# First attention of a decoder layer: keys and values laid out block-diagonally over 64 rows by 64 columns, multiplied in two row strips, with a new job order

## The reference

```python
Q, K, V = proj(Wq, bq), proj(Wk, bk), proj(Wv, bv)   # (n, s, h, d), h = d = 16, after reshape and transpose
scores = jnp.einsum('nqhd,nkhd->nhqk', Q, K) * scale
attn = jax.nn.softmax(scores, axis=-1)
out = jnp.einsum('nhql,nlhd->nqhd', attn, V)
...
x = _layernorm(x + attn_1(x))
x = _layernorm(x + cross_attn(ctx, ctx, x))
x = _layernorm(x + ffn_block(x))                       # attention over the sequence, then 8 experts, top 2
```

## Time and profile before

| | before |
|---|---|
| median of 3 runs | 1203.14 us |
| the profiled execution | 1210.79 us, span 1209.0 us |
| mean granted TensorE clock in it | 0.956 |
| PE / PEld busy | 1082.4 us (90%) / 1015.5 us (84%) |
| DVE, ACT, POOL busy | 810.2, 622.7, 588.4 us |
| first job of phase B on DVE | about 626 us after the start |

### The profile page before, as it was taken

The page is one execution under the profiler, slowest core; times in us unless marked ns, Lnnn a source line. Parts: engine busy times, 40 slices in busy tenths (PEclk is TensorE's granted clock), DMA queues, the critical chain, the costliest instruction groups (busy, mean ns, idle before and its releaser), DMA issues. The chain is left out here.

```text
span 1209.0 us, 32884 instructions
## 1 busy us (share of the span) xinstructions
PE 1082.4 (90%) x13012; PEld 1015.5 (84%) x13012; DVE 810.2 (67%) x1383; ACT 622.7 (52%) x1264; POOL 588.4 (49%) x631
## 2 busy tenths in 40 slices
PE   3799999999999999999728988799999999999981
PEld 2578888899899888898628987799999999999981
DVE  1668877878778778776535432477677767767576
ACT  1245455565555555665422232466666666666443
POOL 4243433433444343334101666267767766766555
PEclk8999999999999999999957988899999999999995
DMA  7585465454555554410058222256766676676265
GB/s 202 97 188 106 80 123 107 90 116 115 108 96 118 116 98 88 86 43 20 28 180 317 88 84 88 100 202 222 244 232 210 226 247 225 217 248 225 86 194 174
DMA packets 288456, 176.37 MB, mean 146 GB/s; under 512 B 213120, under 2 KB 256896, under 8 KB 287680
## 3 DMA queue, kind: packets, MB, share of 16 engines
q1 hardware_dynamic: 277600, 148.90, 46.1%
q0 software_dynamic: 6816, 18.69, 4.3%
q10 hardware_dynamic: 3888, 6.69, 1.5%
HBM read 130.25 MB, written 54.28 MB: 153 GB/s over the span
## 5 line engine op out<-in xcount | busy, mean ns | idle before, releaser
L1395 DVE TENSOR_TENSOR prod<-silu,up 128x512 f32<-128x512 f32 x110 | 75.1, 683 | 161.4 <-ACT silu L1249 139.2
L1379 DVE TENSOR_TENSOR we_lo<-w_raw,we_hi 128x1024 fp32r<-128x1024 f32 x117 | 148.0, 1304 | 15.3 <-ACT we_hi L1233 12.0
L1516 POOL TENSOR_TENSOR act_lo<-prod,act_hi 128x512 fp32r<-128x512 f32 x78 | 100.6, 1290 | 101.5 <-ACT act_hi L1256 101.5
L1524 POOL DMA_INDIRECT routed_scratch<-y_rows,slot_place x78 | 130.9, 1678 | 21.2 <-issue 14.7
L1249 ACT ACTIVATE silu<-gate 128x512 f32<-128x512 f32 x110 | 64.9, 590 | 128.2 <-PE up L1180 98.1
L1233 ACT ACTIVATE we_hi<-w_raw 128x1024 fp32r<-128x1024 f32 x117 | 118.1, 1049 | 21.7 <-DMA w_raw<-in_w_down 21.6
L1256 ACT ACTIVATE act_hi<-prod 128x512 fp32r<-128x512 f32 x110 | 69.6, 632 | 89.4 <-DVE prod L1395 87.5
L668 ACT ACTIVATE p3t<-psum 128x512 f32<-128x512 f32 x128 | 68.7, 596 | 90.8 <-PE psum L517 90.8
L1483 POOL DMA_INDIRECT slots_scratch<-h_rows,slot_index x64 | 65.0, 1016 | 52.5 <-PE up L1180 33.5
L920 POOL TENSOR_TENSOR ctx_lo<-ctx_t,ctx_hi 128x512 fp32r<-128x512 f32 x16 | 20.6, 1286 | 140.3 <-ACT ctx_hi L578 140.3
L839 DVE TENSOR_REDUCE max<-psum 128x16 f32<-128x2048 f32 x32 | 73.3, 2291 | 18.2 <-PE psum L503 18.2
(11 more groups left out here) (264 smaller groups left out, 3322.5 us busy)
## 6 DMA issues: line engine op xcount, KB each, us to landing
w_raw<-in_w_gate SPq DMA_DIRECT2D x40, 512.0 KB
w_raw<-in_w_up SPq DMA_DIRECT2D x40, 512.0 KB
w_raw<-in_w_down SPq DMA_DIRECT2D x40, 512.0 KB
slots_scratch<-in_empty SPq DMA_DIRECT2D x39, 258.0 KB, 3.4
slot_rows<-slots_scratch SPq DMA_DIRECT2D x39, 258.0 KB
w_raw<-routed_scratch SPq DMA_DIRECT2D x32, 256.0 KB, 3.8
x_t<-in_x_t SPq DMA_DIRECT2D x16, 256.0 KB, 3.5
q_scratch<-qk SPq DMA_DIRECT2D x16, 256.0 KB, 2.7
```

Of the source, the lines that this page charges most:

```text
L1379: dve.tensor_tensor(w_lo[:, kind, :], w_raw[:, use % 2, kind, :], w_hi[:, kind, :].bitcast(F32), ALU.subtract).then_inc(w_lo_done, 1)
L1395: dve.tensor_tensor(prod[:, h, :], silu[:, h, :], up[h][:, :], ALU.mult).then_inc(prod_done, 1)
L1516: pool.tensor_tensor(act_lo[:, n % 2, h * FH:(h + 1) * FH, :], prod[:, h, :].rearrange("p (f n) -> p f n", f=FH), act_hi[:, n % 2, h * FH: ...
L1524: pool.indirect_dma_start(out=scratch["routed"], out_offset=bass.IndirectOffsetOnAxis(ap=slot_place[:, i % METAS, j:j + 1], axis=0), in_=y ...
```

## The change

What the diff does, in the first attention alone and in the tables of the order:

1. `kbd` and `vbd` are 64 columns wide instead of 128. Tokens 0 to 3 of a group keep rows 0 to 63 and tokens 4 to 7 rows 64 to 127, and both halves use the same 64 columns.
2. `s1_0` and `s1_1` become one job `s1`, and `o1_0` and `o1_1` one job `o1`. Each has 64 matmuls of 64 rows, 32 stationary columns and 64 streamed columns, in the two strips of 64 rows times four strips of 32 columns. The two row strips write to two different PSUM banks.
3. The evictions follow: `max1`, `sub1`, `o1e` now go by half of a group (a bank) instead of by sequence, with the same number of elements each, and write `p1` in the old layout through a strided view. `exp1`, `t1`, `den1`, `to1` still go by sequence, so each of them waits for both halves.
4. The memsets of `kbd` and `vbd` at the start are half as large, and that of `v3` too (one copy instead of two).
5. `SCHEDULE`, `BANK` and `BUFS` are new for all jobs of phase A. The total lag is the same (7), and PE's largest lag is 6 in both.

```diff
-    for r in range(4):                                      # s1_0, s1_1; the same shape in o1_0, o1_1
-        for j in range(4):
-            g = GB1 * a + 4 * r + j
-            mm = pe.matmul(dst[32 * j:32 * (j + 1), r * P:(r + 1) * P], qc[:, g, :], kbd[:, g, :],
-                           start=True, stop=True)
+    for i in range(2 * 4):                                  # s1; the same shape in o1
+        for half in range(2):
+            for j in range(4):
+                rows, cols = slice(HALF * half, HALF * (half + 1)), 512 * half + HALF * i
+                mm = pe.matmul(dst[32 * j:32 * (j + 1), cols:cols + HALF], qc[rows, 4 * i + j, :],
+                               kbd[rows, 4 * i + j, :], start=True, stop=True)
...
-        kbd = sb("kbd", [P, 2 * GB1, P])
-        vbd = sb("vbd", [P, 2 * GB1, P])
+        kbd = sb("kbd", [P, 2 * GB1, TH * DH])
+        vbd = sb("vbd", [P, 2 * GB1, TH * DH])
...
-                        after(act, f"sub1_{a}", pair)
+                        after(act, "sub1_1", pair)
...
-                        after(pe, f"o1e_{a}", pair)
+                        after(pe, "o1e_1", pair)
...
-BUFS = {"ctx_t": 2, "x_res": 1, "x1": 1, "vo": 1, "x2": 5, "v3": 2}
+BUFS = {"ctx_t": 3, "x_res": 3, "x1": 5, "vo": 2, "x2": 2, "v3": 1}
...
-    "sp": [("load_ctx", 3), ("store_v1", 2), ("store_sum", 7), ("load_k1", 2), ("load_q1", 2), ("load_v1", 2),
-        ("store_q1", 1), ("load_x", 0), ("load_res", 2), ("store_h2", 6), ("store_l", 7)],
+    "sp": [("load_ctx", 2), ("load_x", 0), ("load_v1", 2), ("store_q1", 1), ("store_h2", 6), ("load_res", 0),
+        ("store_v1", 1), ("store_sum", 5), ("store_l", 7), ("load_q1", 1), ("load_k1", 1)],
```

More of the change, by code:

```diff
@@ L96 @@
 }
+TH, HALF = T1 // 2, P // 2
 FAMILIES = [
@@ L101 @@
     ("q3", "k3"), ("q3_0e", "q3_1e", "k3_0e", "k3_1e"),
-    *((f"{n}_0", f"{n}_1") for n in ("s1", "max1", "sub1", "exp1", "den1", "t1", "t1e", "o1", "o1e", "to1", "o1hi", "o1lo",
+    *((f"{n}_0", f"{n}_1") for n in ("max1", "sub1", "exp1", "den1", "t1", "t1e", "o1e", "to1", "o1hi", "o1lo",
                                    "s3", "max3", "tm", "qs", "s3t", "pv3", "o3e")),
@@ L125, in in_order @@
     return [(job, it - lag) for it in range(PAIRS + MAX_LAG) for job, lag in SCHEDULE[engine] if 0 <= it - lag < PAIRS]
-FACTORS_FIRST = next(x for x in in_order("pe") if x[0] in ("s1_0", "vo", "qx"))
+FACTORS_FIRST = next(x for x in in_order("pe") if x[0] in ("s1", "vo", "qx"))
 BEGUN = in_order("pe")[:in_order("pe").index(FACTORS_FIRST)]
@@ L309, in step @@
                         after(sp, "store_q1", pair)
-                        free(sp, "s1_0", pair)
-                        free(sp, "s1_1", pair)
+                        free(sp, "s1", pair)
                         sp.wait_ge(zeros_set, 3)
@@ L315, in step @@
                     elif job in ("load_k1", "load_v1"):
-                        src, dst, users = (("k1", kbd, ("s1_0", "s1_1")) if job == "load_k1" else ("v1", vbd, ("o1_0", "o1_1")))
+                        src, dst, user = ("k1", kbd, "s1") if job == "load_k1" else ("v1", vbd, "o1")
                         if job == "load_k1":
@@ L320, in step @@
                             after(sp, "store_v1", pair)
-                        for user in users:
-                            free(sp, user, pair)
+                        free(sp, user, pair)
                         sp.wait_ge(zeros_set, 3)
@@ L325, in step @@
                         for i in range(T1):
-                            sp.dma_start(dst[DH * i:DH * (i + 1), :, DH * i:DH * (i + 1)], blocks[i]).then_inc(done[job], 16)
+                            sp.dma_start(dst[DH * i:DH * (i + 1), :, DH * (i % TH):DH * (i % TH + 1)], blocks[i]).then_inc(done[job], 16)
                     elif job == "store_sum":
@@ L441, in step @@
                             mm = pe.transpose(dst[:, r * P:(r + 1) * P], p1[:, a, r * P:(r + 1) * P], ident[:, :])
-                    elif job in ("o1_0", "o1_1"):
-                        a = int(job[3])
-                        after(pe, f"t1e_{a}", pair)
+                    elif job == "o1":
+                        after(pe, "t1e_1", pair)
                         after(pe, "load_v1", pair)
-                        for r in range(4):
-                            for j in range(4):
-                                mm = pe.matmul(dst[32 * j:32 * (j + 1), r * P:(r + 1) * P],
-                                               p1t[:, a, r * P + 32 * j:r * P + 32 * (j + 1)], vbd[:, GB1 * a + 4 * r + j, :],
-                                               start=True, stop=True)
+                        for i in range(2 * 4):
+                            for half in range(2):
+                                for j in range(4):
+                                    rows, cols = slice(HALF * half, HALF * (half + 1)), 512 * half + HALF * i
+                                    at = i % 4 * P + 32 * j
+                                    mm = pe.matmul(dst[32 * j:32 * (j + 1), cols:cols + HALF], p1t[rows, i // 4, at:at + 32],
+                                                   vbd[rows, 4 * i + j, :], start=True, stop=True)
                     elif job in ("to1_0", "to1_1"):
                         a = int(job[4])
-                        after(pe, f"o1e_{a}", pair)
+                        after(pe, "o1e_1", pair)
                         for r in range(4):
@@ L584, in step @@
                         a = int(job[4])
-                        free(act, f"o1_{a}", pair)
+                        free(act, "o1", pair)
                         copy_when(job, p1t[:, a, :], bank[f"t1_{a}"], f"t1_{a}", pair)
@@ L759, in step @@
                     elif job in ("max1_0", "max1_1"):
[L760 to L771 removed]
+                        half = int(job[5])
+                        after(dve, "s1", pair)
+                        free(dve, f"sub1_{half}", pair)
+                        dve.tensor_reduce(max1[:, half, :], half_of(bank["s1"], half).rearrange("p (c k) -> p c k", k=H), AX.X,
+                                          ALU.max).then_inc(done[job], 1)
+                    elif job in ("sub1_0", "sub1_1"):
+                        half = int(job[5])
+                        after(dve, f"max1_{half}", pair)
+                        free(dve, "to1_0", pair)
+                        free(dve, "to1_1", pair)
+                        dve.tensor_tensor(half_groups(half), half_of(bank["s1"], half).rearrange("p (i t k) -> p i t k", t=TH, k=H),
+                                          max1[:, half, :].rearrange("p (i t) -> p i t", t=TH).unsqueeze(3).to_broadcast([P, 8, TH, H]),
+                                          ALU.subtract).then_inc(done[job], 1)
                     elif job in ("den1_0", "den1_1"):
```

37 lines of the change are left out of this document (14 added, 23 removed), and 45 rows, old and new, of tables (BANK, LAST_READ, SCHEDULE).

## The result

The changed kernel takes 1227.99 us (median of its runs) beside 1203.28 us for the kernel before on the same chip: 1.020 of before, 95% interval 1.017 to 1.024. On another chip it was 1236.84 beside 1201.17, 1.028 (1.026 to 1.031). The prediction, 1171 us and faster, was wrong. The profiled execution took 1241.95 us and is the slowest of its four, so I read from its trace where the time lies, and the size of it from the ratios; the profiled execution on the other chip, 1237.33 us, shows the same pauses.

What follows compares the result with a forecast made beforehand. PE was taken to bound phase A's steady part: 13 iterations x 1.9 = 25 us, plus 7 us from the start, is 32; 1203.1 - 32 = 1171 us. The 8 in 10 range was 1162 to 1193.

Steps and rivals of the forecast that it cites:

- I charge the order nothing in the steady part: Steady part of phase A: the new job order's waits have cover, so they cost PE 0 us.
- 12 records in 50 ns: PE's instruction rate read from the earlier trace, 4.2 ns each, used as evidence against a floor per instruction.
- a floor per start or per instruction: Rival, chance 0.08: matmul starts or instruction delivery limit the new jobs, a pair loses 3.3 us, about 1239 us.
- 8.3 ns per record: In that rival, the time per PE record above which two new jobs cost what the four cost now.
- The job's price: First attention's matmuls on PE: two new jobs of 1.10 us each, 1.97 us less per pair, taken as 1.9.
- 0.055 to 0.075 us a turn: Range the forecast allowed for a turn of eight tiles in the new jobs; 0.055 is the streaming of 64 columns.
- a bound by instructions: At 12 instructions in 50 ns, a new job's 256 records need 1.07 us instead of 0.87; gain 1.5 per pair.
- How often: Iterations of phase A in which PE is the bound: 13, at 1.9 us each 25 us.
- The strips: Rival, with a wait as alternative, chance 0.12: the two row strips take turns, gain 0.2 us per pair, about 1193.
- The start: Start of phase A: smaller memsets, earlier loads and one fewer job ahead bring the first s1 forward; 7 us kept.
- My lower bound of 2 us: Least gain expected from the start of phase A, from the memsets and one fewer job ahead; upper bound 11 us.
- The end: End of phase A: the chain of the last pair has the same links in both kernels, so no gain taken.

Runs made afterwards that it cites:

- e_spread: The changed kernel with the jobs s1 and o1 each given out in two halves with long jobs between them; 1.041 of before.
- e_products_only: The kernel before, its own orders and banks, with the new products, the lower half of the rows after a wait for the upper; 1.021 of before.
- e_half_instr: The changed kernel with 32 products of 128 columns per job in place of 64 of 64 columns, half the instructions; 0.986 of before.
- e_order_only: The changed kernel's orders, banks and buffer counts, with the first attention's products of the kernel before; 0.998 of before, 1.002 the second time.

## Why the prediction was wrong

**The step that failed** is that the sum has no term for the supply of instructions: "So I charge the order nothing in the steady part", and "12 records in 50 ns" as the argument against such a limit. I looked for waits between jobs and for a rate of records. The rate was there: a job's 256 instructions run in 1.42 us, 5.5 ns each, near the 4.2 ns of the earlier trace rows. What isn't sustained is the refill behind them. From 110.75 to 548.19, 12 iterations take 437.4 us; at the 33.40 of the undisturbed one they would take 400.8. Of the 36.6 us between, 28.0 are gaps at packet boundaries. Five of these gaps, of 2.2 to 3.9 us, are followed by a stretch at 1.2 GHz; at the 1.5 us that one costs in `e_spread` that is an estimate of 7.7. The two make up nearly all.

**The rival** "a floor per start or per instruction" had the right end, and partly by luck. Its 13.6 ns per record, read from a row of before, was no floor of the array: a job takes 1.42 us and not 3.5. But 256 instructions at 13.6 ns are 3.5 us, and the runs show that PE mostly pauses behind 256 in under 3 us, and about every second time behind 256 in 3 to 4. It gave 1232 to 1239; the kernel takes 1228 to 1237, of which a part is the start that gave nothing, and that the rival had at 7 us. I gave it 8 in 100 because I took 50 ns as evidence for 1.4 us. Its 8.3 ns per record, above which the change was to lose, is miscounted: with the 0.23 us for the change of shape and the entry in each job it is 7.2.

**The job's price** was mis-sized, beyond the 0.055 to 0.075 us a turn that the forecast allowed. Less 0.14 for the change of shape, the 1.42 us of a job are 16 turns of 0.080. The streaming that I took, 0.055, is what the array can do: four tiles with 64 columns have a turn every 0.056 us in `e_products_only`, eight tiles with 128 columns every 0.109 in `e_half_instr`, as four had before, and in the changed kernel the second and the third turn of a job come after 0.056 too. The later ones take from 0.066 to 0.148, in the same pattern in every job. At 0.080 a turn has 16 records, 5.0 ns each; I had named a bound by instructions (4.2 ns, 1.07 us a job) and not taken it. That instructions set the later turns fits these numbers, but it wasn't tried by itself. So the new jobs save 4.29 - 2 x (1.42 + 0.09) - 0.12 = 1.15 us per pair, not 1.97. From 34.42 that gives 33.27, and the undisturbed iteration takes 33.40. The 0.3 us by which `e_order_only` is shorter, 34.12, isn't a gain to be added: there `s1` takes 1.77 us for 1.91 and `o1` 1.88 for 2.02, since each has become one job and changes shape once, and this sum has that already.

**How often** it counts I had as 13 iterations; from the fourth `s1` to the last there are 12.

**The strips** do run side by side: eight tiles have a turn in the same 0.109 us as four. That rival is out. The least distance of 25 ns between starts that the Trainium skill gives ("TensorE: Matmul & The Clock Gate", "Wait — 56ns, not 53.3ns?") would make the job 3.2 us; the trace has 11 ns per start over 128 of them, in eight tiles, so it doesn't hold across tiles.

**The start** came as drawn and was not kept. The first `s1` stands at 30.76 where I had 30 to 31. But with the old products in the new order the four first jobs stand at 31.2, 51.7, 75.7 and 106.4, the last where it stood before (106.16), or 1.1 us ahead of it in a second execution: PE waited 7.0 us for `kbd` between them, whose loads take SyncE 6.1 to 8.8 us to issue there against 4.29 in the steady part. The fifth is even later than before, 140.2 for 137.5. My lower bound of 2 us was too high. In the changed kernel the 4.2 us gap at 74.85 is added.

**The end** was right: from the last `s1` to the first load of phase B 108.3 us, 108.2 before.

## What to carry to other kernels

When a change multiplies the number of instructions, count them per microsecond at the densest place and compare with the densest place of a trace that runs without gaps; here the engine mostly stalled behind a packet of instructions used up faster than that, whatever the array could do. Gaps with "issue" as their releaser in the middle of a job, with iterations of changing length, are the sign, and numbering the records shows it, together with the packets of the instruction queue. And an order that brings a first job forward is worth only what the loads behind it can follow: read the fourth or fifth job's start, not the first.

## What the runs showed that was not expected

- Sixteen KB of instructions come in one packet. In the changed kernel TensorE paused at the boundaries between them in 11 of the 13 cases where the 256 instructions ahead had taken under 3 us, and in none of the 64 of before, where they took 4.2 us or more. It went on 1.3 to 2.1 us after a packet had landed. The longest pause was 4.7 us, from start to start.
- The pause depends on other traffic: 3.4 us became 1.3 when seven of eight small-piece loads were left out, and its packet began 2.4 us sooner. Two others stayed within 0.3 us of the first execution's.
- Behind five of the pauses of 2.2 us and more, but not behind one of 2.9, TensorE ran for some 3.4 us at 1.2 GHz. Such a stretch cost 1.5 us.
- In strips of 32 columns, a turn of float32 takes 0.109 us for 128 streamed columns, for four tiles or for eight. For 64 columns it takes 0.056 with four tiles; with eight it starts at 0.056 and has a mean of 0.080 over a job.
- One-column float32 products into one column of PSUM, at the start, moved the first `s1` by 0.28 us each (23 of them by 6.5 us), the first 16 by 8.7 us in all. Why so much wasn't tried.
